# Last experts of a two-layer decoder: weight halves, constants and tables prepared earlier, batch 1's norm and routing ahead of products

## The reference

```python
x = x + _L1_xattn_ref(_layernorm(x), ctx_768, ...)   # 16 heads over 77 context rows; then relu(out @ W1 + b1) @ W2 + b2
x = x + _L1_ffn_ref(_layernorm(x), Wg, W1, W2, Ws1, Ws2)

def _L1_ffn_ref(x, Wg, W1, W2, Ws1, Ws2):            # D = 128, H = 64, E = 16 experts, K = 2
    xf = x.reshape(-1, D)
    scores = softmax(xf @ Wg.T)
    wk, idx = top_k(scores, 2)
    cw = sum(one_hot(idx, E) * wk[..., None], axis=1)
    h = gated(einsum('td,edh->teh', xf, W1))         # gated(y): u, g = split(y); u * silu(g)
    z = einsum('te,teh,ehd->td', cw, h, W2)
    return z + gated(xf @ Ws1) @ Ws2
```

## Time and profile before

| | us |
|---|---|
| median of 3 runs | 698.66 |
| lowest, highest | 698.02, 702.86 |
| the profiled execution, its own time | 694.07 |
| its span in the profile | 692.3 |
| PE busy | 581.7 (84%) |
| DVE busy | 418.8 (60%) |
| ACT busy | 383.8 (55%) |
| POOL busy | 94.7 (14%) |

### The profile page before, as it was taken

How to read it: one execution, slowest core, us unless ns; L and a number is a source line. 1 busy time by engine, 2 the same in 40 slices (tenths; PEclk the granted TensorE clock), 3 DMA queues, 4 the chain that set the end, 5 groups by cost and what they waited for, 6 DMA issues and landing times. The chain is left out here.

```text
span 692.3 us, 9379 instructions
## 1 busy us (share of the span) xinstructions
PE 581.7 (84%) x3281; PEld 316.5 (46%) x3281; DVE 418.8 (60%) x859; ACT 383.8 (55%) x682; POOL 94.7 (14%) x99
## 2 busy tenths in 40 slices
PE   2379899989999687999999996389888857977978
PEld 1112233322333544889998984011222145445756
DVE  8268577567731744645653236878998076537664
ACT  2246867667666356657564430357898713774611
POOL 7200200100001003600000000597000000003000
PEclk9759999999999998999999996568999889997999
DMA  5324200543071502000000000000000002000000
GB/s 157 91 37 57 73 21 2 70 64 52 2 305 26 66 1 94 27 1 1 1 1 3 13 0 1 0 1 1 2 2 2 0 1 94 6 1 0 1 17 15
DMA packets 14785, 22.68 MB, mean 33 GB/s; under 512 B 3524, under 2 KB 9908, under 8 KB 14356
## 3 DMA queue, kind: packets, MB, share of 16 engines
q1 hardware_dynamic: 12916, 15.54, 11.3%
q10 hardware_dynamic: 1824, 6.55, 2.5%
HBM read 9.99 MB, written 0.52 MB: 15 GB/s over the span
## 5 line engine op out<-in xcount | busy, mean ns | idle before, releaser
L536 DVE TENSOR_REDUCE negmax<-ps 128x2 f32<-128x1024 f32 x96 | 113.9, 1221 | 41.0 <-PE ps L467 40.5
L583 ACT ACTIVATE probs<-ps 128x512 f32<-128x512 f32 x192 | 105.9, 598 | 38.6 <-PE ps L486 36.7
L583 ACT ACTIVATE probs_q<-ps,score_scale 128x512 f32<-128x512 f32 x128 | 78.1, 687 | 14.7 <-PE ps L486 13.1
L1857 PEld LDWEIGHTS ps<-experts,hid 128*128 128x128 f32 x640 | 82.7, 191 | 6.9 <-issue 1.0
L1857 PE MATMUL ps<-experts,hid 128*128 128x128 f32 x640 | 84.0, 275 | 0.0
L536 DVE TENSOR_REDUCE negmax_q<-ps 128x2 f32<-128x1024 f32 x64 | 74.7, 1219 | 6.1 <-PE ps L467 5.6
L1934 ACT ACTIVATE hid<-ps 128x512 f32<-128x512 f32 x80 | 47.0, 598 | 48.0 <-PE ps L864 47.9
L864 PE MATMUL ps<-experts,wfc 128*128 128x512 f32 x156 | 49.3, 424 | 0.0
L467 PE MATMUL ps<-gated 64*128 64x512 bf16 x128 | 29.2, 428 | 20.3 <-DMA gated<-parts 9.2
L2028 DVE SCALAR_TENSOR_TENSOR x_tok<-ps,comb,x_tok 128x128 f32<-128x128 f32 x64 | 18.0, 344 | 43.2 <-PE ps L1857 43.2
L500 PE MATMUL ps<-probs_q,v_q 128*32 128x512 f32 x256 | 43.3, 674 | 0.0
(11 more groups left out here) (382 smaller groups left out, 939.7 us busy)
## 6 DMA issues: line engine op xcount, KB each, us to landing
q_wide<-parts SPq DMA_DIRECT2D x12, 256.0 KB, 5.7
k_wide<-parts SPq DMA_DIRECT2D x12, 256.0 KB, 7.0
experts<-in_L_ffn_Wfc_dram ACTq DMA_DIRECT2D x1, 2560.0 KB, 9.5
experts<-in_L_ffn_Wproj_dram ACTq DMA_DIRECT2D x1, 2560.0 KB, 15.8
gated<-parts SPq DMA_DIRECT2D x18, 128.0 KB, 2.4
qs_x<-crossing SPq DMA_DIRECT2D x5, 256.0 KB, 3.0
w<-in_L_ffn_W_dram SPq DMA_DIRECT2D x1, 1024.0 KB, 5.3
square_weights<-in_squares_dram SPq DMA_DIRECT2D x1, 768.0 KB, 7.1
```

The lines of the kernel that those rows point to most:

```text
L536: nc.vector.tensor_reduce(maxima, scores, AX.X, ALU.max, negate=True).then_inc(self.a_max_done, 1)
L583: nc.scalar.activation(self.probs[0:size, g % self.P_SLOTS, :], ps[0:size, self.B_BANK + g % self.B_SLOTS, :], ACT.Exp, scale=scale).then_ ...
L1857: last = nc.tensor.matmul(K.ps[:, y_bank(g), i * P:(i + 1) * P], hid[:, m % SLOTS, i * P:(i + 1) * P], wproj[:, FT * e + f, :], start=(f = ...
```

## The change

- The 9 splits of the up weights move from the end of the last attention and from the experts' loop into the attention's list, as steps ("W", k, 0) behind the B steps 5, 7, ... 21.
- GpSimd's constants (the countdown, `pick`, the zeros of `comb1_parts`) move from the start of the experts' block to the start of the last attention's block; a class `SiluConstants` holds them, and their tiles are now allocated outside the block.
- The dummy activation that brings Silu's table moves from the end of the attention's block to the start of the experts'. New dummy activations bring Sqrt's table ahead of the wait for batch 1's statistics and Exp's ahead of the wait for its scores.
- In the experts, DVE does batch 1's TURN_H at m = 4 (was 5), its softmax and top 2 at m = 7 (was 9), its `combine` at m = 9 (was 10), each ahead of that m's product. ACT does batch 1's exp ahead of silu(7) (was silu(8)).
- PE's wait for the low halves stays only for batch 0.

```diff
@@ HeadsTail
-    EXPERTS = 16
+    EXPERTS, SPLITS = 16, 9
@@ HeadsAttention.extra_scalar
+        if kind == "W":
+            self.tail.split_high(act, b)
@@ HeadsAttention.extra_vector
+        if kind == "W":
+            self.tail.split_low(dve, b)
@@ cross_attention_heads
+    for k in range(tail.SPLITS):
+        extras.setdefault(5 + 2 * k, []).append(("W", k, 0))
...
             att.scalar(act)
-            nc.scalar.activation(K.warm[:, :], K.eps[:, :], ACT.Silu)
-            for k in range(3):
-                tail.split_high(act, k)
+
+        @block.gpsimd
+        def _(pool):
+            ready.make(nc.gpsimd, pool)
...
+class SiluConstants:
...
+    def make(self, ops, eng):
+        self.number(ops)
+        made, pick = Chain(eng, self.made), self.pick
+        made(ops.memset(pick[:, :, :, :].rearrange("p k a d -> p (k a d)"), 0.0))
+        for part in range(3):
+            made(ops.affine_select(out=pick[:, :, :, :], in_=pick[:, :, :, :], compare_op=ALU.not_equal,
+                                   fill=1.0, base=-self.E * part, pattern=[[-2, self.NP_], [-1, 2], [0, 64]],
+                                   channel_multiplier=1))
+        ops.memset(self.parts[:, :, 3 * self.E:self.PARTS], 0.0).then_inc(self.padded, 1)
@@ experts_silu
-    STATS_AT, EXP_AT, COMB_AT = 4, 8, (2, 10)
+    STATS_AT, EXP_AT, COMB_AT = 4, 7, (2, 10)
...
-                pe.wait_ge(tail.n["w_low"], k + 1)
+                if b == 0:
+                    pe.wait_ge(tail.n["w_low"], k + 1)
...
         def _(act):
+            nc.scalar.activation(K.warm[:, :], K.eps[:, :], ACT.Silu)
             tail.scalar(act, 1, tail.TURN, TAIL_BANK[tail.TURN])
             for m in range(M):
                 if m == STATS_AT:
+                    tail.ln.table(act)
                     tail.scalar(act, 1, tail.STATS, None)
                 if m == EXP_AT:
+                    nc.scalar.activation(K.warm[:, :], K.eps[:, :], ACT.Exp)
                     tail.scalar(act, 1, tail.RAW, None)
...
-                if 3 + m <= NP_:
-                    tail.split_high(act, 3 + m)
-
-        @block.gpsimd
-        def _(pool):
-            number(nc.gpsimd)
...
-            tail.split_low(dve, 0)
             softmax(0)
             hot = run(tiles_of(0))
-            tail.split_low(dve, 1)
             step(tail.TURN)
...
-                if m == STATS_AT + 1:
+                if m == STATS_AT:
                     step(tail.TURN_H)
                 if m == 6:
                     step(tail.LOW)
                 if m == 7:
                     step(tail.RAW)
-                if m == EXP_AT + 1:
                     softmax(1)
                     hot = run(tiles_of(1))
-                if m == 10:
+                if m == 9:
                     combine(1, hot)
...
-                if 2 + m <= NP_:
-                    tail.split_low(dve, 2 + m)
```

More of the change, by code:

```diff
@@ L1009, in decoder_kernel @@
                          W["L1_ffn_Wg"])
+        ready = SiluConstants(K, sb)
         with ExitStack() as st:
-            cross_attention_heads(K, sb, st, W, X, tok_a, nc, cross_tiles[1:], tail)
+            cross_attention_heads(K, sb, st, W, X, tok_a, nc, cross_tiles[1:], tail, ready)
         with ExitStack() as st:
-            experts_silu(K, sb, st, W, w2, ws2, out, nc, Q, hid, tail)
+            experts_silu(K, sb, st, W, w2, ws2, out, nc, Q, hid, tail, ready)
 CAUSAL_W = 0.7
@@ L2563, in extra_vector, with cross_attention_heads @@
         kind, b, i = step
+        if kind == "W":
+            self.tail.split_low(dve, b)
         if kind == "Y":
             self.tail.vector(dve, b, i, self.bank_of.get(step))
-def cross_attention_heads(K, sb, st, W, X, tok_a, nc, tiles_of_region, tail):
+def cross_attention_heads(K, sb, st, W, X, tok_a, nc, tiles_of_region, tail, ready):
     NK = CTX_LEN
@@ L2638, in _, with __init__, experts_silu @@
             att.vector(dve)
-def experts_silu(K, sb, st, W, w2, ws2, out, nc, Q, hid, tail):
-    E, NP_ = 16, 8
-    SLOTS, LAG, PARTS = 6, 3, 72
+class SiluConstants:
+    E, NP_, PARTS = 16, 8, 72
+    def __init__(self, K, sb):
+        self.K = K
+        self.parts = sb("comb1_parts", [P, NT, self.PARTS], BF16)
+        self.pick = sb("pick1", [self.PARTS, self.NP_, 2, 64], BF16)
+        self.keys = sb("tmp1", [P, NT, self.E])
+        self.made, self.padded = K.sem("f1_made"), K.sem("f1_padded")
+        self.run, self.chain, self.number = top2(K.nc, K.nc.vector, K, lambda *a: sb(*a[:-1]), None, "f1", self.E, self.keys[:, :, :])
+    def make(self, ops, eng):
[7 more added lines that the diff above has]
+        ops.memset(self.parts[:, :, 3 * self.E:self.PARTS], 0.0).then_inc(self.padded, 1)
+def experts_silu(K, sb, st, W, w2, ws2, out, nc, Q, hid, tail, ready):
+    E, NP_ = ready.E, ready.NP_
+    SLOTS, LAG, PARTS = 6, 3, ready.PARTS
     sg = sb("sg", [P, 3, 512], F32, st)
@@ L2648, in experts_silu @@
     rest = sb("comb1_rest", [P, NT, E], F32, st)
-    parts = sb("comb1_parts", [P, NT, PARTS], BF16, st)
+    parts, pick, tmp = ready.parts, ready.pick, ready.keys
     comb_t = sb("comb1_t", [PARTS, NB * S], BF16, st)
-    pick = sb("pick1", [PARTS, NP_, 2, 64], BF16, st)
-    tmp = sb("tmp1", [P, NT, E], F32, st)
     prob, red = tail.prob, tail.red
     n = {k: K.sem("f1_" + k) for k in ("comb_ready", "comb_turned", "comb_out",
-                                       "made", "padded", "ug_done", "silu_done", "prod_done", "spread", "weighted",
+                                       "ug_done", "silu_done", "prod_done", "spread", "weighted",
                                        "hid_used", "added", "stored")}
@@ L2659, in experts_silu @@
     M = len(work)
-    run, chain, number = top2(nc, nc.vector, K, sb, st, "f1", E, tmp[:, :, :])
+    run, chain = ready.run, ready.chain
     ACC, COMB_BANK = (0, 1), (7, 1)
@@ L2700, in turn_combine @@
             def turn_combine(b):
-                pe.wait_ge(n["made"], 4)
+                pe.wait_ge(ready.made, 4)
                 pe.wait_ge(n["comb_ready"], b + 1)
@@ L2761, in _ @@
                     tail.scalar(act, 1, TAIL[m], TAIL_BANK[TAIL[m]])
-                if 3 + m <= NP_:
-                    tail.split_high(act, 3 + m)
-        @block.gpsimd
-        def _(pool):
-            number(nc.gpsimd)
-            made = Chain(pool, n["made"])
-            made(nc.gpsimd.memset(pick[:, :, :, :].rearrange("p k a d -> p (k a d)"), 0.0))
-            for part in range(3):
-                made(nc.gpsimd.affine_select(out=pick[:, :, :, :], in_=pick[:, :, :, :], compare_op=ALU.not_equal,
-                                             fill=1.0, base=-E * part, pattern=[[-2, NP_], [-1, 2], [0, 64]],
-                                             channel_multiplier=1))
-            nc.gpsimd.memset(parts[:, :, 3 * E:PARTS], 0.0).then_inc(n["padded"], 1)
         @block.sync
@@ L2815, in combine @@
                 chain(nc.vector.tensor_copy(parts[:, t, E:2 * E], rest[:, t, :]))
-                dve.wait_ge(n["padded"], 1)
+                dve.wait_ge(ready.padded, 1)
                 nc.vector.tensor_tensor(parts[:, t, 2 * E:3 * E], rest[:, t, :], parts[:, t, E:2 * E],
```

## The result

The changed kernel takes 686.43 us in the median of 4 runs (684.93 to 690.57), the kernel before 698.34 (693.52 to 702.86). The ratio on record is 0.9862, with a 95% interval of 0.9815 to 0.991; the two medians alone give 0.983. The profiled execution took 685.16 us, its span is 683.4, where before they were 694.07 and 692.3. That one was profiled in the slower of the two states that executions fall into (span 709.6 us); its loop and its rest are as long as those of before, so its parts are used, as the weakest of the evidence.

The account below looks back on a forecast made before the run. Behind 567 us: PE's waits and half clock, until PE runs gapless in the last experts' second half. Terms -2.1 - 8.5 + 0.3 + 1.15 = -9.2 us, to 684.9 profiled, 689.5 on the median; range 684.5 to 696.

Parts of the forecast that it names:

- Batch 1's norm and routing: Last experts: the 1.37 us wait at the transposes goes; routing gains 4.37 + 2.4 (clock) - 0.5 = 6.3 us.
- The end of the attention: Without table load and three splits there, the experts' block begins 0.27 us behind DVE's low half: gain 2.1 us.
- Up(1): Start of the experts: its 1.47 us wait goes, about 0.6 us is given back at half clock.
- Rival D: Clock returns sooner with PE busy without a break, and the attention hides the splits: -11 us, 687.7; chance 0.09.
- the wait of up(1): Start of the experts: 1.47 us for a low half of its weights; GpSimd's slowing gain counted in up(1)'s term.
- The splits in the loop: Attention loop: nine splits delay T's multiply and the next A matmul, 0.3 us lost; bounds nothing to 1.5.
- GpSimd beside the norm: Last attention's norm: constants block DVE's eight `tensor_scalar`, 1.15 us lost; bounds 0 and 2.2.
- rival C: Norm's longer PE pause drops the clock, attention loop starts at half clock; 12 us of it end at 701.5; chance 0.05.
- a low clock anywhere between 570 and 615: Sign in the last attention's norm and loop by which the prediction would be wrong.
- the row against the page: ACT's table loads: trace shows no 1.38 us drain on top of 1.28; by the page, sum about 1 us poorer.

Follow-up runs that it names:

- That one: The kernel before with only GpSimd's constants moved beside the last attention's norm; ratio to before 1.0042 (1.0003 to 1.0081).
- the twelve kernels: The kernel before, the changed kernel and the follow-up kernels, each compared by parts of one profiled execution; ratios to before from 0.9764 to 1.0042.
- the six fillers: Kernel with splits ahead, plus filler matmuls in PE's waits at the attention's end (2, 2, 1, then these 6 last); ratio to before 0.9764.
- splits back: Changed kernel with the 9 splits and Silu's table load at their old places; ratio to before 0.9897.
- order alone: Kernel before with only batch 1's new order in the experts and the dummy loads of Sqrt's and Exp's tables; ratio to before 0.9895.
- late constants: Changed kernel with GpSimd's constants still in the last attention's block, but begun behind the first exp of its loop; ratio to before 0.9818.
- splits ahead: Kernel with late constants, its nine splits moved out of the attention's loop, nearly all ahead of it; ratio to before 0.98.
- nine more fillers: Changed kernel with three more filler matmuls ahead of the norm's transposes and two behind the second, fourth and eighth; ratio to before 0.9851.

## Why the prediction was right

Said were -9.2 us for a profiled execution and 689.5 on the median; measured were -8.9 in the span (-8.15 in the parts that the change can reach) and 686.43. The mechanism of the main term held. That the total came so close is in part luck: the norm cost 1.28 us more than said and the tail gave 0.63 less, the experts gave 1.14 more, and 0.75 of the 8.9 lay ahead of all that was changed. Term by term:

- **Batch 1's norm and routing** were to give 1.37 + 6.3 = 7.7. Undoing them alone costs 7.87, doing them alone gives 7.30. The mechanism holds to the wait that takes the place of the old one: 0.5 said, 0.33 measured, at up(9), for product(7). This one edit is nearly all of the change's gain, and here the prediction was at its best. Its chain from the end of the scores on PE to the end of product(7) was to take 6.6 us against 6.1 that PE had; it took 6.35 (647.60 to 653.95), with the routing at 3.79, as the undisturbed one of before.
- **The end of the attention** was to give 2.1. The splits moved back cost 2.10 in the tail, so the term holds for a clock that falls at one place. The tail of the changed kernel gained only 1.47 on before, because there the clock fell 3 us sooner, which the prediction didn't have. The table load that went into the experts cost nothing seen.
- **Up(1)** was to give 0.87 net (1.47 less 0.6 of half clock). The experts gained 9.64 in all; less 7.87 for the order, 1.77 are left for it, in which the clock's earlier return is contained. I had let up(1) start behind UP_A's modelled end less 0.2, at 5.2 us; it started at 4.37, and the clock was back at 631.0, 4.6 us behind the block's start, not at the 6.1 I took from before. Rival D had named that return; over the twelve kernels it lies between 0.2 and 6.1 us, so the 0.6 that I took off was a guess at a quantity that no edit here was shown to set but the six fillers.
- **Whose the wait of up(1) was** the prediction left half open: the text named the missing low half. The kernel with constants moved alone (no wait), the one with splits back (0.34) and the one with the order alone (1.48) show it: DVE's low half came late since GpSimd blocked the routing in front of it. Either edit by itself ends the wait: with the splits moved and the constants left in the experts up(1) had none either, and began 4.05 us behind the block's start. So the gain can be had only once. The move of the constants gave the experts 1.70 where the splits stayed, and 0.70 where they had moved.
- **The splits in the loop** were put at 0.3 and cost 0.48, in three pairs of kernels alike (27.75 to 27.78 against 27.29 to 27.30). The path is the one named, the multiply of T behind the second split, with waits of 0.29 and 0.39 us at the A matmuls.
- **GpSimd beside the norm** is the term that was mis-sized: 1.15 said, 2.43 measured, beyond the stated bound of 2.2. Of this, 1.46 is what was argued, the `tensor_scalar` that pass GpSimd in pairs; the eighth ended 0.85 us behind the third `affine_select` (572.46), where I had 0.55. The other 0.97 is the clock, which I had set aside as the mild end of rival C. By the prediction's own words a low clock anywhere between 570 and 615 meant that it was wrong, and it was low from 573 to 576: on this term it was wrong. The clock fell in all four kernels with constants in the norm and no fillers, and in one of the seven without them, so they aren't its only cause.

ACT's loads bear out the row against the page. The Trainium skill, "ScalarE: Activation LUTs", section "What ACT_TABLE_LOAD costs", puts a drain of 1.38 us on top of the load at each switch of table, and it isn't seen here, neither behind a load nor ahead of it. In the changed kernel a silu ended at 647.44 and a load began at 647.45, and what followed the load began at 648.75. Another load ran from 640.96 for 1.28 us, and the silu behind it began at 642.26, 0.02 later:

```profile
640.96 1.28 ACT L2788 ACT_TABLE_LOAD   x1
```

The rule of the Trainium skill, "SBUF — State Buffer", section "Who interferes with whom", held for `tensor_scalar`, two of which were blocked in the norm. It has a second rule, for a DVE instruction with two SBUF inputs beside a GpSimd instruction that reads SBUF, and this one held too: in the kernel with late constants such a `tensor_tensor` took 0.82 us instead of 0.42 beside an `affine_select`. The step of 1.04 us in rows 5, which the prediction put to the first rule, is a `tensor_tensor` and belongs to the second. It was right to count the contention against the change: of the changed kernel's four edits this one loses, 2.43 us in the norm for 0.70 in the experts.

Not settled is why the clock falls in the norm of one kernel without constants, why it falls and comes back at another place around the start of the experts from kernel to kernel, and what shortened the loop by 0.25 us with the splits ahead.

## What to carry to other kernels

Work that blocks another engine is not made cheaper by moving it earlier, only by moving it to where the blocked engine isn't on the path: the same constants cost 2.4 us beside a norm (1.5 blocked, the rest the clock that fell), 0.7 under a routing that had slack, up to 1.7 under one that had none, and 0.3 in a loop whose DVE steps mostly read PSUM. Ask of each edit by itself what it gives: here one order of three steps on DVE was worth 7.9 us of 8.2, and the edits beside it nearly cancelled (0.25 us together). Two edits can share one gain, as splits and constants share up(1)'s wait: undo them one at a time and both at once. When a wait is removed, walk the chain to the next product in line; if all its steps have rows, the new wait can be told closely (here 0.5 said, 0.33 measured).

## What the runs showed that I had not expected

- `tensor_scalar` instructions pass GpSimd in pairs: with three `affine_select` of about 1.2 us back to back, the third and the fifth of eight were blocked, two passed from one to the next, and PE's transposes came 2, 2 and 4 with waits of 0.77 us between.
- A filler can buy the clock and give little: six of them took 2.91 us at half clock and brought up(0) from 2.91 to 1.64 us. They ended the block 1.6 us later (tail 19.16 against 17.55) and shortened the experts by 2.2. Whether they would be free in a place where PE rests anyway wasn't tried.
- The half clock comes and goes at other places in stretches of equal code. At the norm it came where the last transposes were 1.5 us late and not with nine more fillers, which looks like a matter of how long PE rests; but it came in "order alone" too, where nothing in the norm differed from before. At the end of the attention it began 12.7 to 17.2 us behind TURN in kernels with equal code there. One profiled execution doesn't tell which of these is the rule, so whoever compares parts should compare the clock of the stretch first.
